# A down projection in seven products per 2x2 blocks, added up by VectorE from PSUM

## The reference

```python
x = x + linear_attention(layernorm(x), ctx, ctx)      # 8 heads, per batch of 128 rows
h = layernorm(x)                                      # 2048 rows of 1024
Wg, Wu, Wd = (NF4[codes] * scales for the three)      # 2752x1024, 2752x1024, 1024x2752
inter = silu(h @ Wg.T) * (h @ Wu.T)                   # 2048 x 2752
out = x + inter @ Wd.T
```

## Time and profile before

| | |
|---|---|
| median of 3 runs | 1581.06 us (1580.51 to 1585.07) |
| profiled execution | 1582.67 us, its span 1581.0 us |
| granted TensorE clock, mean | 0.997 of 2.4 GHz |
| busy: PE / DVE / ACT / POOL | 1560.3 / 479.3 / 847.4 / 60.9 us |
| DMA traffic | 203.51 MB, mean 129 GB/s |
| wide matmuls: gate and up / down | 4128 / 2080 |

### The profile page before, as it was taken

One profiled execution on the slowest core, in us unless ns is written; L12 is line 12 of the kernel. 1 busy time (PEld: TensorE's weight loads), 2 busy tenths in 40 slices (PEclk: granted clock), 3 DMA queues, 4 the chain that ended last, 5 costly groups with the idle time before them and its releaser, 6 DMA issues.

```text
span 1581.0 us, 17409 instructions
## 1 busy us (share of the span) xinstructions
PE 1560.3 (99%) x7296; PEld 1297.2 (82%) x7296; DVE 479.3 (30%) x592; ACT 847.4 (54%) x865; POOL 60.9 (4%) x99
## 2 busy tenths in 40 slices
PE   7999999999999999999999999999999999999999
PEld 6888788888888888888888888888778888888887
DVE  6998321212212222112122122213422224322221
ACT  5777876666666677666666666773211114111110
POOL 3434000000000000000000000000000000000000
PEclk9999999999999999999999999999999999999999
DMA  6553443333334433333333344336663433443340
GB/s 207 170 171 120 158 124 112 113 103 111 93 104 117 120 114 112 100 114 111 104 111 95 100 120 120 114 104 200 226 235 120 150 138 112 150 144 113 143 148 28
DMA packets 96430, 203.51 MB, mean 129 GB/s; under 512 B 7520, under 2 KB 52576, under 8 KB 92512
## 3 DMA queue, kind: packets, MB, share of 16 engines
q1 hardware_dynamic: 96352, 202.41, 40.6%
HBM read 150.99 MB, written 51.38 MB: 128 GB/s over the span
## 4 chain that ended last, share of the span: by engine, by line
PE 92%; ACT 4%; DMA 2%; issue 1%; SPq 1%; DVE 0%; DVEq 0%; ACTq 0%
PE bank L945 20%; PE bank L946 20%; PE bank L947 20%; PE bank L998 9%; PE bank L1000 9%; PE bank L999 9%; PE bank L896 2%; PE bank L923 1%; PE bank L930 1%; PE bank L913 1%; DMA F<-inter_scratch 1%; ACT early L548 1%; SPq L385 1%; ACT F L582 1%; ACT F L567 1%
## 5 line engine op out<-in xcount | busy, mean ns | idle before, releaser
L945 PE MATMUL bank<-R 128*128 128x512 f32 x1376 | 535.9, 389 | 0.0
L946 PE MATMUL bank<-R 128*128 128x512 f32 x1376 | 535.8, 389 | 0.0
L947 PE MATMUL bank<-R 128*128 128x512 f32 x1376 | 535.7, 389 | 0.0
L527 ACT ACTIVATE F<-F 128x1024 f32<-128x1024 f32 x441 | 467.5, 1060 | 13.3
L947 PEld LDWEIGHTS bank<-R 128*128 128x128 f32 x1376 | 258.4, 188 | 53.6
L945 PEld LDWEIGHTS bank<-R 128*128 128x128 f32 x1376 | 258.4, 188 | 53.4
L946 PEld LDWEIGHTS bank<-R 128*128 128x128 f32 x1376 | 258.4, 188 | 53.4
L663 ACT CAST R<-F 128x2816 fp32r<-128x2816 f32 x30 | 76.7, 2557 | 347.5 <-PE bank L1004 321.7
L998 PE MATMUL bank<-R 128*128 128x512 f32 x642 | 250.2, 390 | 2.6 <-DVE R L844 2.6
L1000 PE MATMUL bank<-R 128*128 128x512 f32 x642 | 250.0, 389 | 0.0
L999 PE MATMUL bank<-R 128*128 128x512 f32 x642 | 250.0, 389 | 0.0
(11 more groups left out here) (75 smaller groups left out, 791.4 us busy)
## 6 DMA issues: line engine op xcount, KB each, us to landing
F<-inter_scratch SPq DMA_DIRECT2D x30, 1408.0 KB, 7.5
inter_scratch<-F SPq DMA_DIRECT2D x84, 256.0 KB, 2.4
F<-in_gu_codes SPq DMA_DIRECT2D x41, 512.0 KB, 3.9
F<-in_gu_scales SPq DMA_DIRECT2D x82, 256.0 KB, 3.9
F<-in_d_codes SPq DMA_DIRECT2D x22, 512.0 KB, 3.8
F<-in_d_scales SPq DMA_DIRECT2D x44, 256.0 KB, 3.9
wd_scratch<-F SPq DMA_DIRECT2D x22, 512.0 KB, 4.5
F<-in_x SPq DMA_DIRECT2D x16, 512.0 KB, 3.6
```

The costliest lines, as they stand in the source:

```text
L527: nc.scalar.activation(y, y, ACT.Prelu, bias=bias, scale=scale, alpha=alpha).then_inc(bent, 1)
L945: pe.matmul(dst, hi, xh[:, tb, t, :], start=(t == 0), stop=False)
L946: pe.matmul(dst, hi, xl[:, tb, t, :], start=False, stop=False)
L947: i = pe.matmul(dst, lo, xh[:, tb, t, :], start=False, stop=(t == HT - 1))
```

## The change

The down projection is computed by blocks. A group g takes a pair of token tiles (m, 8 of them) and four inner tiles (r, 5 rounds): `inter` as 2x2 blocks a11, a12, a21, a22 of 128 tokens by 256 inner rows, the weights as 2x2 blocks B11 to B22 of 256 by 512. Seven products (Winograd's form of Strassen's scheme) take the place of eight. The sums of weights (T1 to T4) are formed by VectorE in the gate and up stage (`t_forms`), all seven weight forms are split there (`form_hi` on ScalarE, `form_lo` on VectorE) and stored to `wf_scratch`, hi and lo beside each other; in the down stage they are loaded as they are, 1 MB for each form and round, a round ahead (`load_w`). The sums of `inter` (S1 to S4) are formed by GpSimd from a 512 KB load (`load_stage`), then split (`hi_a`, `hi_s` on ScalarE, `lo_a`, `lo_s` on VectorE).

Products 0, 2, 4 and 6 add up in one bank X, 1 and 5 in Q, 3 in W. The states of a bank are wanted in between: VectorE adds each state to a sum `yacc` in SBUF (which starts as `x1`, 8 loads of 1 MB) before the next product is added onto the bank. The inner tiles 20 and 21 (the last full one and the half one) are done in the last round with 20 matmuls a pair (`rest`), and the outputs are stored from `yacc`, 512 KB at a time. The second half of the output columns is part of the same group; there are no halves left. In gate and up, `store_wd` goes and `store_form` takes its place, and some buffers move in SBUF.

```diff
--- before.py
+++ after.py
...
-    wd_dram = nc.dram_tensor("wd_scratch", (KT, P, N), F32).ap()
+    NP = 7
+    wf_dram = nc.dram_tensor("wf_scratch", (NR, NP, P, 2, 2, WIDE), F32).ap()
+    wr_dram = nc.dram_tensor("wr_scratch", (2, P, N), F32).ap()
...
+        B11, B12, B21, B22 = [v[:, h * WIDE:(h + 1) * WIDE] for v in wdt for h in range(2)]
+        T1, T2, T3, T4 = tform
+        FORMS = [(B11, 0), (B21, 3), (B22, 6), (T1, 4), (T3, 1), (T2, 2), (T4, 5)]
+        KINDS = (2, 0, 3, 1)
...
+        bankX = [banks[0][:, 1, :], banks[3][:, 1, :]]
+        bankQ = [banks[1][:, 1, :], banks[0][:, 0, :]]
+        bankW = [banks[2][:, 1, :], banks[1][:, 0, :]]
+        bankZ = banks[2][:, 0, :]
...
+            def load_stage(g):
+                r, m = g // NM, g % NM
+                for q in range(2):
+                    sp.wait_ge(inter_stored[q], 32 * (4 * r + 4))
+                wait(sp, la_ready, g - 1)
+                wait(sp, s_ready, g - 1)
+                sp.dma_start(stage[g % 2].rearrange("p (t k n) -> p t k n", t=2, k=4),
+                             inter_dram[2 * m:2 * m + 2, :, 4 * r:4 * r + 4, :].rearrange("t p k n -> p t k n")).then_inc(stage_in[g % 2], 16)
+            def load_y(m):
+                sp.dma_start(yacc[:, m], x1_dram[2 * m:2 * m + 2].rearrange("t p n -> p t n")).then_inc(y_in[m], 16)
...
+            load_w(0, 5)
+            load_w(0, 6)
             store_block(FULL, 0, HALF)
+            for m in range(NM // 4):
+                load_y(m)
             store_block(FULL, 1, HALF)
             store_block(FULL, 2, HALF)
             store_block(FULL, 3, HALF)
+            load_stage(1)
+            for m in range(NM // 4, NM):
+                load_y(m)
...
+            for g in range(NG):
+                r, m = g // NM, g % NM
+                if g + 2 < NG:
+                    load_stage(g + 2)
+                if r + 1 < NR and m < NP:
+                    sp.wait_ge(product_done, NP * r * NM + m + 1)
+                    load_w(r + 1, m)
...
+            def s_forms(g):
+                b12, b11, b22, b21 = blocks[g % 2]
+                tt = nc.gpsimd.tensor_tensor
+                pool.wait_ge(stage_in[g % 2], 16 * (g // 2 + 1))
+                if g == 0:
+                    pool.wait_ge(wd_stored, 32)
+                wait(pool, ls_ready, g)
+                tt(S1, b21, b22, ALU.add).then_inc(s_step, 1)
+                tt(S3, b11, b21, ALU.subtract)
+                pool.wait_ge(s_step, 2 * g + 1)
+                tt(S2, S1, b11, ALU.subtract).then_inc(s_step, 1)
+                pool.wait_ge(s_step, 2 * g + 2)
+                tt(S4, b12, S2, ALU.subtract).then_inc(s_ready, 1)
...
+            def form_hi(c, tb):
+                made = form_of(c, tb)
+                if made is None:
+                    return
+                k, _, _, src, _ = made
+                if k % NP < 3:
+                    act.wait_ge(w_ready, 3 * c + 3)
+                else:
+                    act.wait_ge(t_ready, 4 * (k // NP + 1))
+                wait(act, form_stored, 16 * k)
+                nc.scalar.copy(form[0], src).then_inc(fh_ready, 1)
...
+            def hi_a(g):
+                act.wait_ge(stage_in[g % 2], 16 * (g // 2 + 1))
+                wait(act, product_done, NP * (g - 2) + 6)
+                nc.scalar.copy(aform[g % 2][0], stage[g % 2][:, 0:AB]).then_inc(ha_ready, 1)
+            def hi_s(g):
+                act.wait_ge(s_ready, g + 1)
+                wait(act, product_done, NP * (g - 1))
+                nc.scalar.copy(sform[g % 2][0], stemp.rearrange("p (a n) -> p a n", a=2)).then_inc(hs_ready, 1)
...
+            def lo_a(g):
+                dve.wait_ge(ha_ready, g + 1)
+                sub(aform[g % 2][1], stage[g % 2][:, 0:AB], aform[g % 2][0].bitcast(F32)).then_inc(la_ready, 1)
+            def lo_s(g):
+                dve.wait_ge(hs_ready, g + 1)
+                sub(sform[g % 2][1], stemp.rearrange("p (a n) -> p a n", a=2), sform[g % 2][0].bitcast(F32)).then_inc(ls_ready, 1)
...
+            def s1_add(g):
+                if g < NM:
+                    dve.wait_ge(y_in[g], 16)
+                dve.wait_ge(product_done, NP * g + 1)
+                add(part(g, 0, 0), bankX[g % 2]).then_inc(s1_added, 1)
+            def q1_add(g):
+                dve.wait_ge(product_done, NP * g + 2)
+                add(part(g, 1, 1), bankQ[g % 2]).then_inc(q1_added, 1)
+            def s2_add(g):
+                dve.wait_ge(product_done, NP * g + 3)
+                add(part(g, 1, 0), bankX[g % 2]).then_inc(s2_added, 1)
...
+            last_block(0)
+            lo_a(0)
+            last_block(1)
+            last_block(2)
+            dve.wait_ge(gate_done, FULL * TB + TB)
+            lo_s(0)
+            last_block(3)
+            for g in range(NG):
+                r, m = g // NM, g % NM
+                last = r == NR - 1
+                if last and m:
+                    rest_adds(g - 1)
+                elif g:
+                    x_add(g - 1, (product_done, NP * g))
+                s1_add(g)
+                q1_add(g)
+                if g + 1 < NG:
+                    lo_a(g + 1)
+                s2_add(g)
+                if not last:
+                    w_add(g, (product_done, NP * g + 4))
+                if last and m == 0:
+                    for k in range(2):
+                        dve.wait_ge(hrw_ready, k + 1)
+                        sub(restw[k][1], restw_in_f[k], restw[k][0].bitcast(F32)).then_inc(lrw_ready, 1)
+                    lo_rest(0)
+                s3_add(g)
+                if g + 1 < NG:
+                    lo_s(g + 1)
+                if not last:
+                    q2_add(g, (product_done, NP * g + 6))
+                elif m + 1 < NM:
+                    lo_rest(m + 1)
+            rest_adds(NG - 1)
...
-            def tile(g, slot, half, first=False, k0=0):
-                pe.wait_ge(il_ready, g + 1)
-                wait(pe, y_ready, g - 1)
-                dst = banks[slot][:, 0, :]
-                for k in range(k0, KT):
-                    if first:
-                        pe.wait_ge(wdl_ready, half * KT + k + 1)
-                    h, l = (v[slot][:, k * P:(k + 1) * P] for v in (ih, il))
-                    if k < FULL:
-                        pe.matmul(dst, h, wdh[:, k, :], start=(k == 0), stop=False)
-                        pe.matmul(dst, h, wdl[:, k, :], start=False, stop=False)
-                        i = pe.matmul(dst, l, wdh[:, k, :], start=False, stop=False)
-                    else:
-                        pe.matmul(dst, h, wdh[:, k, :], start=False, stop=False)
-                        i = pe.matmul(dst, h, wdl[:, k, :], start=False, stop=True)
-                    i.then_inc(down_step, k0 + 1 if k == k0 else 1)
...
+            def product(g, i, dst, stationary, start):
+                moving = wslot[(g // NM) % 2][i].rearrange("p (q k n) -> p q k n", q=2, k=2)
+                for k in range(2):
+                    h, l = (v[:, k * P:(k + 1) * P] for v in stationary)
+                    pe.matmul(dst, h, moving[:, 0, k, :], start=start and k == 0, stop=False, skip_group_check=not start)
+                    pe.matmul(dst, h, moving[:, 1, k, :], start=False, stop=False, skip_group_check=not start)
+                    last = pe.matmul(dst, l, moving[:, 0, k, :], start=False, stop=k == 1, skip_group_check=not start)
+                last.then_inc(product_done, 1)
...
+            for g in range(NG):
+                r, m, b = g // NM, g % NM, g % 2
+                x, q, w2 = bankX[b], bankQ[b], bankW[b]
+                a12, a11, a22 = [[aform[b][h][:, i * BK:(i + 1) * BK] for h in range(2)] for i in range(3)]
+                s1, s2, s3, s4 = [[sform[b][h][:, i // 2, i % 2 * BK:(i % 2 + 1) * BK] for h in range(2)] for i in range(4)]
+                in_place = 16 * (r + 1)
+                pe.wait_ge(la_ready, g + 1)
+                wait(pe, x_added, g - 1)
+                if m == 0:
+                    pe.wait_ge(w_in[0], in_place)
+                product(g, 0, x, a11, True)
+                pe.wait_ge(ls_ready, g + 1)
+                wait(pe, q2_added, g - 1)
+                if g == 1:
+                    pe.wait_ge(up_copied, 2)
+                if m == 0:
+                    pe.wait_ge(w_in[1], in_place)
+                product(g, 1, q, s3, True)
+                pe.wait_ge(s1_added, g + 1)
+                if m == 0:
+                    pe.wait_ge(w_in[2], in_place)
+                product(g, 2, x, s2, False)
+                wait(pe, w_added, g - 1)
+                if m == 0:
+                    pe.wait_ge(w_in[3], in_place)
+                product(g, 3, w2, a12, True)
+                pe.wait_ge(s2_added, g + 1)
+                if m == 0:
+                    pe.wait_ge(w_in[4], in_place)
+                product(g, 4, x, s1, False)
+                pe.wait_ge(q1_added, g + 1)
+                if m == 0:
+                    pe.wait_ge(w_in[5], in_place)
```

(30 more changed lines are left out.)

541 lines of the change are left out of this document (248 added, 293 removed).

## The result

The changed kernel took **1540.84 us** (median of four runs, 1540.18 to 1542.58) against 1581.17 before: ratio 0.974, 95% interval 0.972 to 0.976. The forecast was 1545, its own range 1537 to 1553. The profiled execution took 1541.15 us, its span is 1539.4, 41.6 less than before; the sum had 35.8.

The account below looks back on a forecast made before the run. The prediction took both stages to be bound by the number of matmuls on TensorE. Its terms summed to -35.8 us, from the profiled 1582.67 to 1546.9, or 1545 us as median; own range 1537 to 1553, overall 1531 to 1567.

Parts of the forecast that it names:

- Matmuls: Down projection: 1840 matmuls instead of 2080, 240 fewer at an unchanged 0.2268 us each, -54.4 us.
- Gate and up: Gate and up stage: extra casts, subtractions and form stores fit into idle time, +0 us, ends 0 and 20.
- Steady groups: Down projection's steady groups: 0.08 us a group lost between VectorE's instructions, +3 us, ends 0 and 26.
- no slack at product 4: Each steady group: `s2` released at 5.45 us, wanted at 5.44, so further VectorE delay there costs its full length.
- the rivals on VectorE: Down projection groups: slower VectorE adds, 1562 us, chance 17%; or GpSimd's forms holding VectorE up, 1592 us, 8%.
- Start of the down projection: Entry to the down stage: TensorE waits for late loads of stages 1 and 2, then half clock, +12.4 us.
- Last round: Group 32: two 1024-column splits and a small one ahead of `s3` on VectorE delay its product, +1.2 us.
- End: After the last matmul: the last store is 512 KB rather than 256, +2 us, ends 0 and 4.5.
- Start of the stage: Up to the first down matmul, at 1102.91 us: the same times as before expected, 0 us.
- the cheap entry: Start of the down projection: faster or earlier loads cut its cost to 0 to +4, 1532 us; chance 14%.
- gates that miss: Steady groups: VectorE takes 0.3 to 0.9 us more between `q1` and `s2`, 1562 us; chance 17%.
- GpSimd does hold VectorE up: Steady groups: GpSimd's forms overlap `lo_a` and one waits for the other, 1.3 us a group, 1592 us; chance 8%.

Follow-up runs that it names:

- e4: Changed kernel with product 3 done twice in each group, 240 matmuls more, loads, forms and adds unchanged: 1592.39 us.
- e8: Changed kernel with every weight form stored to DRAM twice, the second copy read by nobody: 1543.70 us.
- e5: Changed kernel with `lo_a` computed twice in every group, still ahead of the `s2` add on VectorE: 1574.70 us.
- e10: Changed kernel with two unused GpSimd additions, 128x512 and 128x384, at the head of its forms in every group: 1548.86 us.
- e1: Changed kernel with the load of stage 2 issued ahead of the six 1 MB x1 loads instead of behind them: 1533.54 us.
- e11: Changed kernel with four of the six x1 loads issued later, in the groups, one behind each stage load: 1534.23 us.
- e9: Changed kernel with stage 1 and 2 loads issued earlier, `s2` add before `lo_a`, and four of six x1 loads later, in the groups: 1528.93 us.
- e7: Changed kernel with two unused 128x512 GpSimd additions at the head of its forms in every group: 1543.66 us.
- e6: Changed kernel with `lo_a` moved behind the `s2` add and computed twice in every group: 1545.55 us.

## Why the prediction was right

Term by term, in span, forecast and measured:

- **Matmuls: -54.4, -54.4.** The pace stayed at 0.2268; e4 gives the count back and with it the time.
- **Gate and up: 0, 0.** The window and e8 bear out the cover. The casts waited 6.0 us for the stores of the forms in all (the row of L677 above), where the prediction had about 1 us for each of 70.
- **Steady groups: +3, 0.** This is the term that was wrong, with the claim of no slack at product 4 behind it. `lo_a` comes 0.61 us behind the start of an add of 0.69, and `s2`'s add 0.87 behind the start of a `lo_a` of 0.95:

```profile
1396.32 0.69 DVE L922 TENSOR_TENSOR early<-early,bank 128x512 f32<-128x512 f32 x1 [0.67 <-PE bank L1108]
1396.93 0.95 DVE L852 TENSOR_TENSOR R<-F,R 128x768 fp32r<-128x768 f32 x1
1397.80 0.68 DVE L922 TENSOR_TENSOR early<-early,bank 128x512 f32<-128x512 f32 x1
```

  Consecutive instructions of VectorE overlap by 0.08 us here; I had summed their lengths and added 0.03 between them. `s2` ends at 5.07 into the group, not 5.29, and the gate has some 0.2 us of slack, 0.16 to 0.18 by e5 and e10. The Trainium skill (Perfetto Trace Analysis, Optimizing Scalar/DVE Operations) says that part of an instruction's recorded length, the write's acknowledgement, overlaps the next instruction; these rows agree. That a delay beyond the slack costs its full length, the base of the rivals on VectorE, holds.
- **Start of the down projection: +12.4, +12.9** (13.7 up to product 4 of group 1, 2.1 of half clock behind it, less the 2.9 us that the down stage before had over its bare matmuls). Stage 1 was forecast for 1110.3 and landed at about 1109.3, stage 2 for 1128.6 and landed at 1127.2; product 4 of group 1 started at 1130.16, forecast 1131.3. e1 and e11 show the cause. The half clock cost 2.1, not 1.6. Two waits between VectorE and GpSimd stand in this chain (`lo_a` took 1.35 us at 1110.27 and again at 1128.16), 0.4 us each that the prediction did not have.
- **Last round: +1.2, +0.6.** The same overlap on VectorE; one gap of 0.57 us at 1430.86. **End: +2, +0.7.** The span ends 4.33 us after the last matmul starts, before 3.62: the two stores of 512 KB landed 2.6 and 2.8 us after their issue, where 4.5 was taken from the earlier trace rows.
- **Start of the stage: 0, -1.4.** The first down matmul starts at 1101.54, not 1102.91; 0.6 of it is already there at the first gate matmul, and 0.8 is one gap of TensorE at 170 us, 1.4 us from start to start before and 0.6 now. Both are within what the start varies by between executions, so nothing of it is put down to the change.

These sum to -41.6. The terms at fault are small and, but for 0.5 us at the entry, on one side: 4.4 us of cost that did not come, net, and 1.4 at the start, which is luck. Of the rivals, the cheap entry did not come in this kernel, but e9 is very nearly it (1532 forecast, 1528.9); gates that miss cost 0.84 us for 1.00 us of delay (e5). GpSimd does hold VectorE up (e10), but the rival's condition was wrong: it let `lo_a` wait for all four forms once they end later than 3.6 us into the group, 1.3 us a group. `lo_a` waits for the one that is running at most: in e7 the forms end at 5.9 and a group costs nothing more, in e10 at 5.5 and it costs 0.21. In the changed kernel its forms (0.74 to 0.77 us, forecast 0.73) end over 1 us before `lo_a` in the steady groups.

## What to carry to other kernels

Where an algorithm takes matmuls away from a TensorE that is the bound, count the matmuls first, and then look where the other engines' first data of the new stage stand in the DMA queue: here six loads, of which the first was needed 32 us after its issue and the last 77 us after, cost 7 of the 16 us lost in the down stage (e11). In VectorE's queue it was the place of an instruction that cost, not its length: the same 0.95 us cost 0.84 a group ahead of a gate and 0.06 behind it. Add up VectorE's instructions from start to start, not by their lengths, and keep those that read two operands from SBUF apart in time from GpSimd's.

## What the runs showed of the hardware

- **The clock after a pause.** In the down stages of all these runs, every pause of TensorE from 2.4 to 7.1 us was followed by matmuls at 0.43 us from start to start, 1.2 GHz, and none from 0.4 to 1.5 us was. Between them the length alone does not decide: a pause of 1.96 us (e8, first three rows) was followed by a fall, one of 2.33 us (e6, last three) was not, and what decided is not shown.

```profile
1106.37 0.51 PE L1108 MATMUL bank<-FR 128*128 128x512 f32 x1 [1.96 <-DVE early L924]
...
1107.25 0.63 PE L1108 MATMUL bank<-FR 128*128 128x512 f32 x1
1107.67 0.63 PE L1109 MATMUL bank<-FR 128*128 128x512 f32 x1
```

```profile
1433.41 0.50 PE L1108 MATMUL bank<-R,FR 128*128 128x512 f32 x1 [2.33 <-DVE early L924]
1433.75 0.40 PE L1109 MATMUL bank<-R,FR 128*128 128x512 f32 x1
1433.99 0.39 PE L1110 MATMUL bank<-R 128*128 128x512 f32 x1
```

  Nor was the slow stretch of one length: behind the pauses of 2.4 us and more it ended 2.7 to 6.1 us after the resumption and cost 1.4 to 3.0 us against the full pace, without order by the length of the pause, where the estimate from the earlier trace rows was 1.6.
- **The lock between VectorE and GpSimd acts by the whole instruction, in both directions,** and which one pays depended on a shift of 0.3 us (e7 against e10). A kernel may run free of it by luck and lose 6 us by an edit that only shifts GpSimd.
- **A load waits for what was queued before it on SP**: the same 0.5 MB landed 18.0 us after its issue behind 6 MB of x1, at a mean of 386 GB/s (changed kernel), 9.0 us behind 2 MB (e11) and 4.6 us when it was issued ahead of all six loads (e1).
